# A two-layer token pipeline: squares halved and decay parts split on VectorE, step sizes two stages sooner, GpSimd's state sums behind its queries

## The reference

```python
# 1. selective state space model: 256 channels, 8 states
xc = silu(causal_conv4(x_in) @ pw + conv_bias)         # x_in, z = split(x @ W_in)
delta = softplus(x_dbl[..., :8] @ W_dt + b_dt)         # x_dbl = xc @ W_x; B, C are its other columns
h = exp(delta * A) * h + delta * B_t * xc;  y_t = sum_n C_t * h      # a scan over 512 tokens
out = ((y + xc * D) * silu(z)) @ W_out
# 2. x @ sign(weight).T
# 3. gated linear attention: 16 heads of 64
s = exp(g_t) * s + k_t^T v_t;  o_t = q_t s             # k is gated; g = -softplus(x @ Wd.T + bd)
out = (rmsnorm(o over 1024 features) * norm_w * sigmoid(x @ Wog.T)) @ Wo.T
# 4. mixture of experts: top 2 of 8, a gated hidden layer of 512 each
```

## Time and profile before

| | |
|---|---|
| median of 3 runs | 2577.02 us (2574.51 to 2595.25) |
| profiled execution | 2582.14 us, span 2580.3 us |
| PE busy | 2221.5 us, 86% |
| DVE busy | 1871.7 us, 73% |
| ACT busy | 1469.4 us, 57% |
| POOL busy | 813.6 us, 32% |
| first transpose of x2_new (round 2 opens) | 126.55 us |
| last transpose of x2_new (round 17 opens) | 1979.11 us |

### The profile page before, as it was taken

The page is one execution under the profiler, slowest core; times in us unless marked ns, Lnnn a source line. Parts: engine busy times, 40 slices in busy tenths (PEclk is TensorE's granted clock), DMA queues, the critical chain, the costliest instruction groups (busy, mean ns, idle before and its releaser), DMA issues. The chain is left out here.

```text
span 2580.3 us, 53740 instructions
## 1 busy us (share of the span) xinstructions
PE 2221.5 (86%) x16824; PEld 1658.7 (64%) x16825; DVE 1871.7 (73%) x3521; ACT 1469.4 (57%) x3336; POOL 813.6 (32%) x1092
## 2 busy tenths in 40 slices
PE   3489898999889898989898989899989939999990
PEld 1247565666657565757575757575757739999990
DVE  2796869685968686777777786869685437777778
ACT  2276666665666566666666666667665603333334
POOL 0112414141414141414142323233242323334346
PEclk9599999998999899999999999999989969999995
DMA  4531414141423232323132223324140032222216
GB/s 121 119 90 43 103 38 99 41 97 40 97 58 84 53 83 68 79 61 87 51 87 66 71 66 71 86 52 98 39 107 5 10 132 58 59 57 56 60 46 195
DMA packets 144122, 189.19 MB, mean 73 GB/s; under 512 B 16984, under 2 KB 92768, under 8 KB 143552
## 3 DMA queue, kind: packets, MB, share of 16 engines
q1 hardware_dynamic: 121680, 118.72, 15.9%
q0 software_dynamic: 22272, 67.92, 12.4%
HBM read 109.77 MB, written 27.56 MB: 53 GB/s over the span
## 5 line engine op out<-in xcount | busy, mean ns | idle before, releaser
L1407 DVE TENSOR_TENSOR_SCAN hs<-decay,push 128x512 f32<-128x512 f32 x256 | 351.2, 1393 | 26.0 <-ACT decay L1069 20.5
L1156 ACT ACTIVATE S<-banks,fall_tok 128x128 f32<-128x128 f32 x1024 | 278.5, 385 | 28.4 <-PE banks L786 28.4
L978 PE MATMUL banks<-rowsT,w_here 128*128 128x128 f32 x2176 | 269.3, 277 | 7.3 <-DVE w_here L1731 7.3
L1512 DVE SCALAR_TENSOR_TENSOR oT<-tog,banks 128x512 f32<-128x512 f32 x128 | 87.6, 684 | 243.5 <-ACT sq L1123 243.3
L978 PEld LDWEIGHTS banks<-rowsT,w_here 128*128 128x128 f32 x2176 | 255.9, 193 | 10.7 <-issue 9.8
L1505 DVE TENSOR_TENSOR S<-banks,S 128x512 f32<-128x512 f32 x256 | 170.8, 687 | 104.2 <-PE banks L798 98.0
L1810 POOL DMA_DIRECT2D y<-ch x96 | 88.7, 924 | 498.8 <-DVE ch L1415 397.3
L1908 POOL TENSOR_TENSOR qd<-q,qd 128x512 f32<-128x512 f32 x96 | 134.1, 1397 | 292.0 <-ACT qd L1141 292.0
L1951 POOL DMA_INDIRECT results_scratch<-rows_out,result_to x136 | 132.3, 973 | 241.1 <-ACT rows_out L1285 234.4
L1274 ACT ACTIVATE tanh_h<-banks 128x512 f32<-128x512 f32 x136 | 81.3, 598 | 203.7 <-PE banks L978 203.7
L1069 ACT ACTIVATE decay<-delta,a_neg 128x512 f32<-128x512 f32 x256 | 171.9, 729 | 17.7 <-DVE hs L1407 17.1
(11 more groups left out here) (221 smaller groups left out, 5361.2 us busy)
## 6 DMA issues: line engine op xcount, KB each, us to landing
y<-ch POOLq DMA_DIRECT2D x96, 512.0 KB, 6.2
b_all<-bc_scratch SPq DMA_DIRECT2D x128, 256.0 KB, 5.5
c_all<-bc_scratch SPq DMA_DIRECT2D x128, 256.0 KB, 3.6
rows_in<-rows_scratch SPq DMA_DIRECT2D x136, 66.0 KB
both<-results_scratch SPq DMA_DIRECT2D x32, 256.0 KB, 3.5
w<-w_dram SPq DMA_DIRECT2D x3, 2048.0 KB, 8.9
x_tok<-x_dram SPq DMA_DIRECT2D x16, 256.0 KB, 3.3
x_again<-x_dram SPq DMA_DIRECT2D x16, 256.0 KB, 2.9
```

Source lines behind the costliest of these rows:

```text
L978: mm = pe.matmul(bank_h[:, u % 2, n, here], w_here[:, u % 2, n, here], x, start=True, stop=True)
L1156: ins = nc.scalar.activation(S[:, g, here], bank[:, here], ACT.Exp, bias=fall_tok[:, head:head + 1])
L1407: nc.vector.tensor_tensor_scan(hs[:, h, :], decay[:, n % 2, h, :], push[:, h, :], 0.0, ALU.mult, ALU.add).then_inc(s_scan, 1)
```

## The change

Five things change:

1. `project_out` sums half as many squares on TensorE: VectorE first adds the two halves of each `sq` tile (`sq_less`, a 128x256 addition behind each `gate_out`, eight a round), so that L878 has 4 products for 8 (8 instructions for 16), four times a round. `project_out` waits for `sq_less`.
2. `fall_less` moves from GpSimd to VectorE, in units 3 and 4, behind k.
3. The step sizes move from stage 6 to stage 4 (matmuls and ScalarE's `steps`) and from stage 7 to stage 5 (`step_sizes`); the gate z moves from stage 5 to stage 6 and waits for `step_sizes`, as both use `th`. This also changes the order of the bank ring.
4. On GpSimd the sums of states 4, 5 and 6 come behind `decay_queries`, `rms_of` and `send_rows` of their stage.
5. Buffers: x_again is gone, its load goes straight into x1 and waits for the previous sequence's `ffn` bank (stage 6) instead of `mix` (stage 4). `take` writes a new x2_kept and needs no wait for the scatter; that wait moves to the first `residual` on VectorE (stage 3). `store_x3` comes one state later on SyncE.

```diff
-FRONT = {"xT": 0, "u0": 1, "u1": 2, "xdbl": 3, "z0": 5, "z1": 5, "dt0": 6, "dt1": 6}
-SIZES_STAGE, BC_STAGE, TAKE_STAGE, X3_AFTER = 7, 3, 2, 3
+FRONT = {"xT": 0, "u0": 1, "u1": 2, "xdbl": 3, "dt0": 4, "dt1": 4, "z0": 6, "z1": 6}
+SIZES_STAGE, BC_STAGE, TAKE_STAGE, X3_AFTER = 5, 3, 2, 4
...
# SyncE
-                        drained(sp, ring, i - 1, "mix")
-                    sp.dma_start(x_again[:], x_dram[bass.ds(i, 1)].rearrange("b p c d -> (b p) c d")
+                        drained(sp, ring, i - 1, "ffn")
+                    sp.dma_start(x1[:], x_dram[bass.ds(i, 1)].rearrange("b p c d -> (b p) c d")
...
# TensorE, project_out
                 pe.wait_ge(s_og, at(j, STAGES, 2 * c + 2))
+                pe.wait_ge(s_sq_less, at(j, STAGES, 2 * c + 2))
...
-                for t in range(PAIRS):
-                    mm = pe.matmul(bank[:, P:P + 1], sq[:, t // 4, t % 4 * P:(t % 4 + 1) * P], ones[:, 0:1],
-                                   start=(t == 0), stop=(t == PAIRS - 1))
+                for t in range(PAIRS // 2):
+                    mm = pe.matmul(bank[:, P:P + 1], sq_less[:, t // 2, t % 2 * P:(t % 2 + 1) * P], ones[:, 0:1],
+                                   start=(t == 0), stop=(t == PAIRS // 2 - 1))
...
# ScalarE
             def gate_input(h, n):
                 bank = full(ring, f"z{h}", n)
-                act.wait_ge(s_xc, at(n, HALVES, h + 1))
+                act.wait_ge(s_delta, at(n, HALVES, HALVES))
...
-                drained(act, ring, n, "dt0", "dt1", "z0", "z1")
+                drained(act, ring, n, "dt0", "dt1")
+                act.wait_ge(s_xc, at(n, HALVES, HALVES))
...
-                if not first(j):
-                    act.wait_ge(s_x3_stored, at(j, 16, 0))
-                    act.wait_ge(ring.full_sem("x3T"), ring.full_at("x3T", j))
-                    act.wait_ge(s_scattered, at(j, 16 * 2 * TILES, 0))
-                nc.scalar.copy(x3[:], x2_new[:]).then_inc(s_x2_taken, 1)
+                after(act, s_residual, at(j, TILES, 0))
+                nc.scalar.copy(x2_kept[:], x2_new[:]).then_inc(s_x2_taken, 1)
...
# VectorE
+            def fall_less(n, j):
+
+                dve.wait_ge(s_fsplit, at(j, 5, 2 * n + 1))
+                if n == 0:
+                    nc.vector.tensor_tensor(fall_rest[:], fall[:], fall_parts[:], ALU.subtract).then_inc(s_fsplit, 1)
...
# gate_out
+                nc.vector.tensor_tensor(sq_less[:, f, :], sq[:, f, 0:2 * P], sq[:, f, 2 * P:4 * P], ALU.add
+                                        ).then_inc(s_sq_less, 1)
...
# body
                         if u == FALLS:
                             log_decay(j)
+                        if u in FALL_PARTS[:2]:
+                            fall_less(FALL_PARTS.index(u), j)
...
# GpSimd, stage
                 m = STATE_IN_STAGE.get(h) if i is not None else None
-                if m is not None and m <= SUMS:
-                    sum_state(m, i)
                 if j is not None:
...
                 if i is not None:
+                    if m is not None and m <= SUMS:
+                        sum_state(m, i)
```

More of the change, by code:

```diff
@@ L316, in build @@
         x_tok = sb("x_tok", [P, TILES, P])
-        x_again = sb("x_again", [P, TILES, P])
         xT = sb("xT", [P, TAPS - 1 + T])
@@ L334, in build @@
         x2_new = sb("x2_new", [P, TILES, P])
+        x2_kept = sb("x2_kept", [P, TILES, P])
         x2T = sb("x2T", [P, T])
@@ L362, in build @@
         sq = sb("sq", [P, 2, T])
+        sq_less = sb("sq_less", [P, 2, 2 * P])
         mixed = sb("mixed", [P, 2, P + 1])
@@ L462, in build @@
         s_og = sem("o_gated")
+        s_sq_less = sem("squares_halved")
         s_half_state = sem("state_first_half")
@@ L1201, in stage @@
                         parameters(n)
+                    if h == FRONT["dt1"]:
+                        steps(n)
                     for half in range(HALVES):
@@ L1204, in stage @@
                             gate_input(half, n)
-                    if h == FRONT["dt1"]:
-                        steps(n)
                 if j is not None:
@@ L1462, in add_mixed @@
                 dve.wait_ge(s_x_again, at(i, 16, 16))
-                nc.vector.tensor_tensor(x1[:], full(ring, "mix", i).rearrange("p (t d) -> p t d", d=P), x_again[:],
+                nc.vector.tensor_tensor(x1[:], full(ring, "mix", i).rearrange("p (t d) -> p t d", d=P), x1[:],
                                         ALU.add).then_inc(ring.free_sem("mix"), 1)
@@ L1494, in log_decay @@
                                                  ALU.mult, ALU.add).then_inc(s_fall, 1)
+            def fall_less(n, j):
+                dve.wait_ge(s_fsplit, at(j, 5, 2 * n + 1))
+                if n == 0:
+                    nc.vector.tensor_tensor(fall_rest[:], fall[:], fall_parts[:], ALU.subtract).then_inc(s_fsplit, 1)
+                else:
+                    nc.vector.tensor_tensor(fall_rest[:], fall_rest[:], fall_parts[:], ALU.subtract).then_inc(s_fsplit, 1)
             def project(u, j):
@@ L1521, in residual @@
                     dve.wait_ge(s_x2_taken, at(j, 1, 1))
+                    if not first(j):
+                        dve.wait_ge(s_x3_stored, at(j, 16, 0))
+                        dve.wait_ge(ring.full_sem("x3T"), ring.full_at("x3T", j))
+                        dve.wait_ge(s_scattered, at(j, 16 * 2 * TILES, 0))
                 nc.vector.scalar_tensor_tensor(x3[:, c, :], mixed[:, c % 2, 0:P], rms[:, c:c + 1],
-                                               x3[:, c, :], ALU.mult, ALU.add).then_inc(s_residual, 1)
+                                               x2_kept[:, c, :], ALU.mult, ALU.add).then_inc(s_residual, 1)
             def decay_keys(h, j):
@@ L1589, in stage @@
                 if n is not None:
+                    if h == SIZES_STAGE:
+                        step_sizes(n)
                     for half in range(HALVES):
@@ L1592, in stage @@
                             gate_input(half, n)
-                    if h == SIZES_STAGE:
-                        step_sizes(n)
             diagonal = [(slice(n * DH, (n + 1) * DH), slice(n * DH, (n + 1) * DH)) for n in range(2)]
@@ L1827, in _ @@
             wide = [P, TILES, EXPERTS]
-            def fall_less(n, j):
-                pool.wait_ge(s_fsplit, at(j, 5, 2 * n + 1))
-                if n == 0:
-                    nc.gpsimd.tensor_tensor(fall_rest[:], fall[:], fall_parts[:], ALU.subtract).then_inc(s_fsplit, 1)
-                else:
-                    nc.gpsimd.tensor_tensor(fall_rest[:], fall_rest[:], fall_parts[:], ALU.subtract).then_inc(s_fsplit, 1)
             def find_rows(j, it):
@@ L1935, in body @@
                             closing(u, j - 1, j)
-                        if u in FALL_PARTS[:2]:
-                            fall_less(FALL_PARTS.index(u), j)
                 for h in range(STAGES):
```

## The result

| | |
|---|---|
| median of the changed kernel | 2564.62 us (2559.97 to 2571.32, 17 runs) |
| median of the kernel before, beside it | 2587.04 us (2562.53 to 2611.83, 17 runs) |
| ratio | 0.9932, 95% interval 0.9912 to 0.9951 |
| profiled execution | 2564.62 us, span 2562.8 us |

The change makes the kernel 0.7% faster. 2537 us was forecast against 2577 us, which is 1.55%; 2564.6 lies in the range of 2512 to 2572, but the gain is 0.7% where 1.55% was forecast, and "within 1%" had been given a chance of 0.29.

A forecast was written before the change was run, and what follows sets the result against it. TensorE bounds the stages, VectorE units 3 to 7. Terms -3.4 + 0.4 - 1.4 + 0.15 + 0.5 + 1.25 = -2.5 us a round, times 16 is -40 us: 2542 against the profiled 2582.14, median 2537 us; range 2512 to 2572.

The forecast's parts named there:

- within 1%: Outcome of a time from 2551 to 2603 us, not told from no change; chance 0.29.
- Buffers … Nothing for all three.: SyncE's later x1 load with transfers behind it, `take`'s lost wait and later `store_x3` cost nothing.
- Squares, TensorE's side: L878 in stages 2, 4, 6 and unit 0: eight instructions fewer save 0.86 us each time, -3.4 us a round.
- Squares, VectorE's side: `sq_less` additions of 0.33 us on VectorE delay stages 1 and 2: +0.4 us a round, ends 0.2 and 1.4.
- Decay parts: Units 3 to 7: VectorE's scans no longer stall beside GpSimd's subtractions, -1.4 us a round, bounds -2.0 and +1.2.
- Races in stages 1 and 2: GpSimd's `qd` beside `ch` and `push` of state 5, half the rounds at 1.3 us: +0.15 us, ends -0.5 and +1.3.
- Step sizes sooner: ScalarE's extra work in stage 4 delays `sq(4)`; TensorE waits at stage 5's scores: +1.25 us a round, ends 0 and 3.
- Sums behind queries: State 6's sum lands in y near 1331, before `gate_state` in stage 3 wants it; covered by 1 us, cost 0.
- The gain is given back in the stages: Rival, 0.24: lost `qd` races, ScalarE's pile-up in stages 4 to 6 and `sq_less` eat the gain; 2560 us (2551 to 2577).
- Lands late: Rival, 0.08: state 6's sum lands 5.8 us late, `gate_state` in stage 3 waits, +2.3 us a round, 2614 us.
- TensorE keeps its clock: Rival, 0.06: a shorter wait in unit 5 keeps TensorE's clock up, -4.3 us a round, 2508 us.
- The forecast's own list of what would prove it wrong: TensorE's waits in stages 0 to 6 up over 2 us a round, `gate_state` waiting, or `fall_less` awaiting ScalarE over 1 us.

The follow-up runs named there:

- The experiment: Sixteen products at L878 again and no `sq_less`, against the changed kernel with the load of x1 back early in its own buffer: 2571.14 us, 0.9955.
- An edit that took 0.34 us of waiting a round away: `sq_less` moved behind the next `add_update`, against the changed kernel with step sizes late and only x1's load late: 2528.16 us, 0.9809.

## Why the prediction was off, step by step

**What failed: "Buffers … Nothing for all three."** The forecast saw that six transfers of 256 KB would start together behind the wait for stage 6, and asked only whether their data would come in time. They do. It did not ask what else goes on at the moment at which they run. They run into the jump, where TensorE's instructions have to come in as well, and there they cost 22 us by the ratios, a term of +1.4 us a round that the sum had at nothing. The forecast could not see either that halved squares bring one more instruction transfer next to the jump. The kernel with the load put back runs in 2540.36 us where the forecast said 2537, with 120.4 us from opening to opening on average (121 was forecast; the changed kernel has 122.0). This step is the gap. That the rest then fits to a few microseconds is partly luck, as its terms were off by up to 0.5 us a round in both directions (below).

**Squares, TensorE's side: right.** L878's line has become 8 instructions, with 0.81 us from its start to the next matmul (timeline of PE, stage 4; the earlier trace rows has 1.71 us):

```profile
1576.05 0.95 PE L881 MATMUL banks<-ones,sq_less 128*128 128x1 f32 x8
1576.86 1.14 PE L852 MATMUL banks<-qd,state 128*128 128x128 f32 x8
```

**Squares, VectorE's side: right in sum, and one wait is shared.** `sq_less` takes 0.41 us, 0.33 from start to start, as taken. It was charged with 0.4 us for stages 1 and 2 and 0.5 for stage 4. The experiment shows 0.33 in each of stages 1 and 2 and about 0.1 in stage 4, so 0.8 for 0.9. The 0.83 us in stage 5 go away both without `sq_less` and without the sooner step sizes. They need both, and the forecast had charged them to the step sizes alone. With them halving is worth 1.9 us a round, without them 2.7, for 2.5. In stage 4 VectorE did what the forecast described: `qd` starts just ahead, `sq_less` is held (DVE, then POOL). But TensorE wanted the state only some 0.1 us before it came:

```profile
1566.05 1.30 DVE L1526 TENSOR_TENSOR sq_less<-sq 128x256 f32<-128x256 f32 x1
```

```profile
1565.81 1.26 POOL L1917 TENSOR_TENSOR qd<-q,qd 128x512 f32<-128x512 f32 x1 [6.48 <-ACT qd L1145]
```

**Decay parts: right mechanism, size 0.9 for 1.4.** The scan pairs of units 3 and 5 take 2.34 us, and the mean of 1250 ns lies in the 1230 to 1300 that was forecast. But VectorE's gain is not all TensorE's: of the waits for k, two of 1.47 us stay in every round.

**Races in stages 1 and 2: wrong in kind.** The forecast took half the rounds at 1.3 us, and kept "each one lost" as the upper end. Each one is lost, in stage 1 and in stage 2, at 1.08 and 1.94 us over a `push` of 1.22 us. Against before, `push` loses 42 us of VectorE's time in all (330 ns by 128) and xc gives back 19 (587 ns by 32). On TensorE's path little of it arrives. The wait in stage 2 was 1.38 us in five of the middle rounds and is 1.40 in all of them; by the kernel with whole squares 1.06 us of that is not `sq_less`. The reordering as such is a gain of 4 to 8 us, 0.25 to 0.5 us a round, where +0.15 was taken.

The Trainium skill (SBUF — State Buffer, section "SBUF: two separate sides") says that a VectorE operation with two SBUF inputs and one of GpSimd lock each other out. The lengthened `push` and `sq_less` beside `qd` agree with it. By the same section the one that starts first has the ports; here a `push` that starts 0.43 us ahead of `qd` was held all the same, and so was xc in the earlier trace rows, 0.20 us ahead.

**Step sizes sooner: right in size, the make-up in part by luck.** 1.25 us a round was taken, 20 us in all, and 20 us is what undoing it gives back: 13 us of it the shared wait in stage 5, 6 us TensorE's busy time, which the forecast had not counted. The order on ScalarE is the forecast one, Ln, `sq(4)` and the table load behind it (timeline of ACT, stages 4 and 5):

```profile
1578.58 1.06 ACT L1065 ACTIVATE th<-th 128x1024 f32<-128x1024 f32 x1
...
1579.69 0.60 ACT L1127 ACTIVATE sq<-banks 128x512 f32<-128x512 f32 x1
1580.31 1.28 ACT L1144 ACT_TABLE_LOAD   x1
```

and the wait behind it, 0.83 us at 1582.44, lies in the 0.7 to 0.95 us that were given.

**Sums behind queries: right.** The sum of state 6 leaves at 1555.41 and VectorE's `y` starts at 1563.05 without a wait.

**The rivals.** "The gain is given back in the stages" named the right time, 2560 us, for the wrong reason: each race was lost, but that cost TensorE little, and ScalarE's pile-up cost what the sum had for it. "Lands late" did not happen. "TensorE keeps its clock" did not either: the mean granted clock went from 0.935 to 0.941 only, and the opening now comes at half clock. The forecast's own list of what would prove it wrong looked at stages 0 to 6 and at two waits of VectorE, never at the opening, which it had put at the same 3.18 us before and after.

**The sum of the parts.** Undone one at a time from the kernel with the early load, the parts are worth 31 (squares), 14 (parts), -20 (step sizes) and 4 us (sums), which is 29; the kernel gained 40. Most of the 11 us left is the shared wait of stage 5, which is counted against both the squares and the step sizes: 0.83 us in sixteen rounds are 13 us, and counted once the parts add up to 42. What the later `store_x3` and `take`'s lost wait are worth was not tried alone. Against the forecast's terms, with the shared wait at the step sizes as there: squares 44 us for 40, parts 11 to 14 for 22, step sizes -20 for -20, sums 4 to 8 for -2. The errors nearly cancel, which is the luck in the fit.

## What to carry to other kernels

When a load moves behind a later wait, look up what its queue holds behind it, when all of that will then run, and what it will run beside: in these kernels the hardware loop's jump was a bad neighbour, as the instructions of the next round come in by DMA too. Bursts should have landed before it, or only the one transfer that needs the late buffer should wait. An edit that only takes instructions away can move an instruction transfer next to the jump, so the DMA view around the jump is worth a look after every edit. A wait that two edits cause together is to be charged to the pair, and a race between engines that an edit of order ends at one instruction is to be looked for at the one before or behind it.

## What the runs showed of the hardware

- TensorE stands still for 2.5 to 3.3 us at each jump of this loop when little traffic is under way. With a burst of 1.5 MB that reaches up to 2.5 us into the pause it was 4.0 to 5.7 us in the changed kernel (6.3 us once with GpSimd's sums first), and 2.8 to 3.8 us in the kernel before.
- The end of the pause follows the landing of the last 16 KB instruction transfer by 1.6 to 2.5 us, in all 192 jumps. Alone, such a transfer takes 0.9 to 1.5 us; of two beside the burst, the later one mostly took 1.5 to 2.3 us. That they wait behind the data is read from their starts (in the changed kernel -0.3 to 1.3 us and 0.1 to 2.5 us into the pause, with the load early -1.8 to -1.7 and 0 to 0.6), not from a run that moved them alone.
- A lost race holds the two-input operation for about its rival's whole length or a little more, even where the rival began later: in the earlier trace rows xc starts 0.20 us ahead of `qd` and takes 2.38 us, and here a `push` that starts 0.43 us ahead of a `qd` of 1.65 us takes 3.16 us for 1.22.
- An edit that took 0.34 us of waiting a round away went with a lower clock: 24 us more busy time for the same 16184 instructions of TensorE, and 0.937 to 0.942 granted in its four runs for 0.947 to 0.951. Why is not known.
